# A new slot table for the delta stage of a decoder layer

## The chip, the cores and the metric

The kernel runs on one core of a Trainium2 chip. The core has a matrix engine (TensorE, PE in the profile), a vector engine (VectorE, DVE), an activation engine (ScalarE, ACT), a general engine (GpSimd, POOL) and an engine that issues most transfers (SyncE, SP). Each runs its own instruction list in order and waits on semaphores for the others. The metric is the device time of one execution in microseconds (us); lower is better.

## The reference

The input is x, 4 batches of 1024 tokens of width 256, in float32. One decoder layer is computed: a gated delta-rule attention, a cross attention to a short context, and a mixture of 8 experts with 2 per token, each followed by a layer norm. The change touches only the first part. For every batch and head (4 heads, keys of 64, values of 128) it keeps a state S of 64 x 128 and goes through the tokens:

```python
def _step(S, inp):
    q_t, k_t, v_t, g_t, b_t = inp
    S = S * jnp.exp(g_t)[..., None, None]
    v_eff = (v_t - jnp.einsum('bhk,bhkv->bhv', k_t, S)) * b_t[..., None]
    S = S + k_t[..., None] * v_eff[..., None, :]
    o_t = jnp.einsum('bhk,bhkv->bhv', q_t, S)
    return (S, o_t)
...
o = o * jax.lax.rsqrt(jnp.mean(o * o, -1, keepdims=True) + EPS) * norm_w
o = o * g_out * jax.nn.sigmoid(g_out)
return x + o.reshape(B, T, DV) @ Wo
```

## The kernel before

The kernel is a row of stages with a barrier between them: projections (to about 306 us of the span), the delta stage (to about 872 us), the context, cross attention, experts and the last norm. The delta stage works on chunks of 128 tokens, 8 chunks per batch, the 4 batches side by side. Inside a chunk the recurrence is turned into matrix products with the inverse of a unit triangular 128 x 128 matrix per head.

There is work of two kinds. **Front work** does not need the state. For a chunk it is: turning q and k (`new`, L856; ACT copies them to qkT at L1010), the products k k^T (L834, `kk`), E, the decays between tokens (POOL writes its diagonal at L770, VectorE scans at L1083), PK = kk x E (L1138), the inverse of PK, and PQ = q k^T x E (L834 for `qq`, L1159). The inverse starts with 16 x 16 diagonal blocks: PK's blocks go through DRAM (`lanes`, L692 and L697) to N16, VectorE inverts them (L1101 to L1130), the result goes back through DRAM (`image`, L709, L716, L717) to T and U. Then TensorE doubles the block size in two levels of three groups each: Z (L887, masked by VectorE at L1165), Y (L901, subtracted at L1173) and X (L911, copied by ACT at L1018 or L1022); the last doubling is z6 (L918, copied at L1178) and y6 (L925, copied at L1028).

**The state step** of a batch b in a chunk is the tail: `state_keys` (PE, L941), `targets` (DVE, L1184), `updates` (PE, L949), `updates_out` (ACT, L1034), `outputs` (PE, L957, L961, L967), `new_state` (DVE, L1193), `squares` (ACT, L1041, L1045), `gated` (DVE, L1200, L1205), `gated_turned` (PE, L975), `gated_out` (ACT, L1050), `projected` (PE, L981), `residual` (DVE, L1215 to L1220), `deviations` (ACT, L1054), `norm_terms` (DVE, L1224, L1226), `normed` (ACT, L1058) and `store` (POOL, L798). The PSUM banks A and B exist twice, so batch b uses the pair b % 2, and `state_keys` of b waits until `residual` of b - 2 has read it.

The order on every engine is written out by `run`: a chunk has 16 slots, and in slot f each engine first issues `ready(f)` for chunk c + 1, then `new(f)` for chunk c + 2, then the tails of the four batches for chunk c, then `rest(f)` for chunk c + 2.

```python
for b in sorted(G, key=lambda b: -((f - 4 * b) % SLOTS)):
    n = c - (f < 4 * b)
    if 0 <= n < CHUNKS:
        tail((f - 4 * b) % SLOTS, n, n % 2, b)
```

So batch b starts its step in slot 4b, and a tail phase p of batch b falls into slot 4b + p; of the phases that meet in one slot the oldest batch goes first. Phases 0, 1 and 2 on TensorE are state keys, updates and outputs; in before phase 5 turns the gated output and phase 6 projects it. `ready` and `new` place the front work by slot numbers; `rest` holds the scans and the base inverse.

## Time and profile before

| what | value |
|---|---|
| median of 3 runs | 1945.23 us (1943.38 to 1946.1) |
| the profiled execution | 1951.58 us, of which the span is 1949.8 us |
| TensorE busy in the span | 81% |
| VectorE busy | 59% |
| ScalarE busy | 41% |
| GpSimd busy | 30% |
| granted TensorE clock, mean over the span | 0.893 |

The durations below come from the one profiled execution; the medians come from runs without a profile. Start times are in us from the span's start. A busy TensorE counts the matmuls in flight and is not TensorE at its peak.

### The profile page before, as it was taken

Reading aid. Unit: us, or ns where it says so; the run is one execution under the profiler, and the core shown is the slowest. Engines: PE = TensorE matmul, PEld = TensorE weight load, DVE = VectorE, ACT = ScalarE, POOL = GpSimd, SP = SyncE. Lnnn points to the kernel's source line nnn. Section 1 sums busy time; section 2 is a strip of 40 time slices with the busy share of each in tenths; the row PEclk is TensorE's granted clock in tenths of the full one; section 3 lists DMA queues with packets and bytes.
Section 4 is the critical chain, followed back from the end, with each engine's and each line's share of the span. In section 5 each row is a group of like instructions: output and inputs, shape, how many; then the busy total and the mean of one; then the engine's idle time right before and its main releaser. Section 6 shows DMA issues by size and latency. Waiting matters only on the chain. (4 is left out here: it accounts for less than half of the span.)

```text
span 1949.8 us, 31224 instructions
## 1 busy us (share of the span) xinstructions
PE 1575.8 (81%) x10722; PEld 1115.3 (57%) x10722; DVE 1151.8 (59%) x2425; ACT 807.7 (41%) x1715; POOL 589.1 (30%) x515
## 2 busy tenths in 40 slices
PE   5898982279889898856589999999746999999980
PEld 3444441267778777743347777676633666666650
DVE  4998983356676676323235677777753555554545
ACT  3777771023343434322345555555312333333324
POOL 0222224122132321001023355454542333333330
PEclk9898985578899889977799999999868999999995
DMA  2232326545355543102610222310321111111117
GB/s 83 86 141 85 141 85 163 139 98 140 83 141 149 133 125 96 55 14 104 232 52 32 88 74 76 116 34 23 125 103 29 46 47 47 45 47 48 44 39 261
DMA packets 189896, 178.73 MB, mean 92 GB/s; under 512 B 88392, under 2 KB 148476, under 8 KB 189628
## 3 DMA queue, kind: packets, MB, share of 16 engines
q1 hardware_dynamic: 175131, 149.75, 25.5%
q0 software_dynamic: 10400, 22.95, 3.6%
q10 hardware_dynamic: 4224, 4.19, 0.6%
q8 instruction: 84, 1.38, 0.3%
q14 instruction: 57, 0.46, 0.1%
HBM read 116.73 MB, written 60.11 MB: 91 GB/s over the span
## 5 line engine op out<-in xcount | busy, mean ns | idle before, releaser
L533 DVE SCALAR_TENSOR_TENSOR conv_y<-conv_in,taps,conv_y 128x512 f32<-128x512 f32 x192 | 165.5, 876 | 20.3 <-ACT conv_y L401 15.7
L2231 POOL DMA_INDIRECT y<-o,idx x71 | 83.4, 1175 | 241.9 <-DVE o L2374 234.2
L2310 ACT ACTIVATE xsT<-pX 128x256 f32<-128x256 f32 x71 | 27.3, 384 | 303.7 <-PE pX L2255 303.7
L1674 PE MATMUL xQ<-late,last 128*128 128x512 f32 x256 | 125.3, 612 | 16.5 <-ACT late L1830 7.9
L2266 PE MATMUL pG<-w_gu,xsT 128*128 x284 | 135.5, 600 | 1.3 <-issue 0.6
L2287 PE MATMUL pD<-late,hT 128*128 x568 | 134.2, 379 | 0.0
L2266 PE MATMUL pU<-w_gu,xsT 128*128 x284 | 133.8, 593 | 0.0
L322 PE MATMUL ps_j<-xnT,w_qkv 128*128 128x512 f32 x256 | 132.5, 655 | 0.0
L1640 POOL TENSOR_TENSOR sc<-sc,den 128x1232 f32<-128x1232 f32 x32 | 71.9, 2248 | 174.6 <-DVE den L2056 174.5
L2287 PEld LDWEIGHTS pD<-late,hT 128*128 128x128 f32 x568 | 102.5, 190 | 11.0
L2370 DVE TENSOR_TENSOR o<-pD,late 128x256 f32<-128x256 f32 x71 | 30.2, 425 | 120.8 <-PE pD L2287 120.8
L1634 POOL TENSOR_TENSOR sc<-sc,madd 128x1232 f32<-128x1232 f32 x32 | 82.6, 2581 | 46.1 <-DVE sc L2038 46.1
L2266 PEld LDWEIGHTS pU<-w_gu,xsT 128*128 128x128 f32 x284 | 54.2, 191 | 68.7 <-issue 68.7
L265 POOL TENSOR_TENSOR sq<-tok 128x1024 f32<-128x1024 f32 x16 | 34.2, 2135 | 195.5 <-ACT tok L391 195.5
L2356 DVE TENSOR_TENSOR u<-pU,last 128x512 f32<-128x512 f32 x71 | 49.1, 692 | 67.3 <-issue 50.2
L1625 POOL DMA_INDIRECT list<-ent,idx x64 | 71.3, 1113 | 53.0 <-DVE ent L1995 36.7
L322 PEld LDWEIGHTS ps_j<-xnT,w_qkv 128*128 128x128 f32 x256 | 52.3, 216 | 55.1 <-issue 55.1
L2222 POOL DMA_INDIRECT xs<-x,idx x71 | 68.3, 962 | 45.1 <-DVE idx L2348 24.7
L790 POOL TENSOR_TENSOR ke<-qk,gbt 128x256 f32<-128x256 f32 x32 | 25.7, 804 | 179.8 <-DVE S L1193 179.7
L1674 PEld LDWEIGHTS xQ<-late,last 128*128 128x128 f32 x256 | 45.1, 191 | 59.7 <-issue 31.2
L981 PE MATMUL psAB<-w_o,u 128*128 128x256 f32 x256 | 77.1, 454 | 0.8 <-ACT u L1050 0.8
L1728 PE MATMUL xO<-vw,aT 128*128 128x256 f32 (+1 forms) x320 | 75.6, 393 | 2.3 <-DVE x2t L2066 1.2
(317 smaller groups left out, 3745.2 us busy)
## 6 DMA issues: line engine op xcount, KB each, us to landing
qkvg<-tok SPq DMA_DIRECT2D x8, 2048.0 KB, 6.7
qkvg<-gate SPq DMA_DIRECT2D x8, 1024.0 KB, 8.8
step<-step SPq DMA_DIRECT2D x32, 256.0 KB, 3.8
qk<-qkvg SPq DMA_DIRECT2D x32, 256.0 KB, 4.2
vb<-qkvg SPq DMA_DIRECT2D x32, 256.0 KB
gt<-qkvg SPq DMA_DIRECT2D x32, 256.0 KB
y<-y SPq DMA_DIRECT2D x16, 512.0 KB
xin<-in_x SPq DMA_DIRECT2D x11, 512.0 KB, 4.0
```

Of the source, the lines that this page charges most:

```text
L322: mm = pe.matmul(ps_j[j % 2][:], w_qkv[:, c, j * P:(j + 1) * P], xnT[b][:, c, :], start=c == 0, stop=c == KD - 1)
L533: y = nc.vector.scalar_tensor_tensor(conv_y[m % 4][:], conv_in[b][:, m, k:k + BT], taps[:, m, k:k + 1], conv_y[m % 4][:], ALU.mult, ALU.add)
L981: mm = pe.matmul(B[b % 2][:, 0:D], ogT[b][:, k, :], w_o[:, head(k), :], start=k == 0, stop=k == H - 1)
L1625: nc.gpsimd.indirect_dma_start(out=s["list"], out_offset=bass.IndirectOffsetOnAxis(ap=idx[:, k, t:t + 1], axis=0), in_=ent[:, t, k, :], in ...
L1634: nc.gpsimd.tensor_tensor(v, v, madd[b % 2][:].unsqueeze(1).broadcast_to([P, XH, CTX]), ALU.add).then_inc(masked, 1)
L1640: nc.gpsimd.tensor_tensor(v, v, over_keys(den[g % 2][:]), ALU.mult).then_inc(scaled, 1)
L1674: mm = pe.matmul(Q[:], w_q[:, c, j * P:(j + 1) * P], x1T[:, c, :], start=c == 0, stop=c == KD - 1)
L1728: mm = pe.matmul(O[:, (g % 2) * D:(g % 2 + 1) * D], aT[g % 2][0:rows(c), c, :], vw[b % 2][0:rows(c), c, :], start=c == 0, stop=c == KCH - 1)
L2222: nc.gpsimd.indirect_dma_start(out=xs[q][:], out_offset=None, in_=s["x2"].rearrange("t p d -> (t p) d"), in_offset=bass.IndirectOffsetOnAx ...
L2231: nc.gpsimd.indirect_dma_start(out=s["y"].rearrange("t p d -> (t p) d"), out_offset=bass.IndirectOffsetOnAxis(ap=idx[j % 8][:, 0:1], axis= ...
L2266: mm = pe.matmul(to[:], xsT[q][:, c, :], w_gu[:, bass.ds(e, 1), c, k * FF:(k + 1) * FF], start=c == 0, stop=c == KD - 1)
L2287: mm = pe.matmul(pD[q][:, 0:D], hT[q][:, k, :], w_d[:, bass.ds(e, 1), k, :], start=k == 0, stop=k == FK - 1)
```

## The change

Nothing is computed otherwise, and no buffer is added. Slots and phases are renumbered, and the waits between engines are set to the new order:

| work | slot or phase before | after |
|---|---|---|
| qq products and PQ (c + 1) | 1 | 0 |
| qk turned and copied (c + 2), batches 0, 1 / 2, 3 | 2 / 4 | 1 / 2 |
| kk products and PK (c + 2) | 5 | 4 |
| Z, Y, X of level 4 (c + 1) | 3, 7, 8 | 5, 6, 8 |
| Z, Y, X of level 5 | 9, 10, 11 | 9, 10, 12 |
| scans of the four batches | 1, 2, 3, 4 | 0, 1, 2, 3 |
| base inverse (m = 1, 2, 4, 8) | 8, 9, 9, 10 and 11 | 8, 8, 9, 10 and 11 |
| diagonals out, in; inverses out | 6, 8; 11 | 5, 7; 12 |
| loads of the next scores | 5, 9, 13, 15 | 4, 8, 11, 15 |
| gated output turned, copied | phase 5 | phase 6 |
| projected and residual | phase 6 | phase 7 |
| deviations, norm terms, normed, store | 7, 8, 9, 10 | 8, 9, 10, 11 |

The waits: turning qk of the second pair now waits on PQ of the chunk before (before: on Z), kk no longer waits on Z, Z of level 4 waits on PK of the next chunk for all batches, and Y of level 4 no longer does.

```diff
@@ -634,7 +634,7 @@
         at = lambda c, b: c * BATCH + b + 1
         LEVS, SLOTS = (4, 5), 16
         lat = lambda c, lev, b: (c * len(LEVS) + lev - LEVS[0]) * BATCH + b + 1
-        Z_AT, Y_AT, X_AT = {3: 4, 9: 5}, {7: 4, 10: 5}, {8: 4, 11: 5}
+        Z_AT, Y_AT, X_AT = {5: 4, 9: 5}, {6: 4, 10: 5}, {8: 4, 12: 5}
         FIRST, SECOND = (0, 1), (2, 3)
         flat = lambda t: t[:].rearrange("p k j -> p (k j)")
         lanes, image = s["lanes"], s["image"]
@@ -725,11 +725,11 @@
                 load_scores(b, c + 1 + b * CHUNKS)
 
             def new(f, c, par):
-                if f == 6:
+                if f == 5:
                     diagonals_out(c, par)
-                if f == 8:
+                if f == 7:
                     diagonals_in(c)
-                if f == 11:
+                if f == 12:
                     inverses_out(c)
                 if f == 15:
                     inverses_in(c)
@@ -737,8 +737,8 @@
                         for b in G:
                             load_values(b, 0)
                             load_gates(b, 0)
-                if c + 1 < CHUNKS and f in (5, 9, 13, 15):
-                    next_scores((5, 9, 13, 15).index(f), c)
+                if c + 1 < CHUNKS and f in (4, 8, 11, 15):
+                    next_scores((4, 8, 11, 15).index(f), c)
 
             def tail(f, c, par, b):
                 if c + 1 == CHUNKS:
@@ -746,7 +746,7 @@
                 if f == 1:
                     sp.wait_ge(w_done, at(c, b))
                     load_values(b, c + 1)
-                if f == 7:
+                if f == 8:
                     sp.wait_ge(x_sum, at(c, b))
                     load_gates(b, c + 1)
 
@@ -798,19 +798,16 @@
                 pool.dma_start(s["x1"][c + b * CHUNKS], x1t[b][:]).then_inc(x1_out[b], 16)
 
             def new(f, c, par):
-                if f == 1 and c:
+                if f == 0 and c:
                     for b in G:
                         diagonal(c, b)
                 if f % 4 == 3:
                     if c:
                         key_ends(c, f // 4, par)
-                    if f > 3:
-                        decayed(c, f // 4, par)
-                if f == 4:
-                    decayed(c, 0, par)
+                    decayed(c, f // 4, par)
 
             def tail(f, c, par, b):
-                if f == 10:
+                if f == 11:
                     store(c, b)
 
             for b in G:
@@ -843,28 +840,23 @@
                     round_of(pair, 1).then_inc(done, 1)
 
             def new(f, c, par):
-                if f in (2, 4):
-                    for b in (FIRST, SECOND)[f // 4]:
+                if f in (1, 2):
+                    for b in (FIRST, SECOND)[f - 1]:
                         pe.wait_ge(qk_in[b], c * 80 + 80)
                         if c:
-                            if b in FIRST:
-                                pe.wait_ge(pq_done, at(c - 1, b))
-                            else:
-                                pe.wait_ge(z_sb, lat(c - 1, LEVS[0], b))
+                            pe.wait_ge(pq_done, at(c - 1, b))
                             pe.wait_ge(qkg_done, at(c - 1, b))
                         for k in range(4):
                             mm = pe.transpose(M[b][:, k * P:(k + 1) * P], qk[b][:, k * P:(k + 1) * P], ident)
                         mm.then_inc(qkT_done, 1)
-                if f == 5:
+                if f == 4:
                     def free(pair):
                         pe.wait_ge(qkT_sb, at(c, pair[1]))
-                        if c and pair == FIRST:
-                            pe.wait_ge(z_sb, lat(c - 1, LEVS[0], pair[1]))
 
                     products(c, 1, free, kk_half, kk_done)
 
             def ready(f, c, par):
-                if f == 1:
+                if f == 0:
                     def free(pair):
                         pe.wait_ge(pk_done, at(c, pair[1]))
                         if c:
@@ -876,8 +868,8 @@
                     for b in G:
                         if lev == LEVS[0]:
                             pe.wait_ge(t_in, c * 16 + 16)
-                            if b in FIRST and c + 1 < CHUNKS:
-                                pe.wait_ge(qkT_sb, at(c + 1, b))
+                            if c + 1 < CHUNKS:
+                                pe.wait_ge(pk_done, at(c + 1, b))
                             else:
                                 pe.wait_ge(pq_done, at(c, b))
                         else:
@@ -894,8 +886,6 @@
                         pe.wait_ge(z_sb, lat(c, lev, b))
                         if lev == LEVS[0]:
                             pe.wait_ge(u_in, c * 16 + 16)
-                            if c + 1 < CHUNKS:
-                                pe.wait_ge(pk_done, at(c + 1, b))
                         for k in range(H):
                             for r in HALF:
                                 mm = pe.matmul(M[b][half(r), P + k * (HP // 2):P + (k + 1) * (HP // 2)],
@@ -989,9 +979,9 @@
                     updates(c, par, b)
                 if f == 2:
                     outputs(c, par, b)
-                if f == 5:
+                if f == 6:
                     gated_turned(c, b)
-                if f == 6:
+                if f == 7:
                     projected(c, b)
 
             run(new, ready, tail)
@@ -1002,8 +992,8 @@
             act.wait_ge(set_up, 3 + 3 * BATCH)
 
             def new(f, c, par):
-                if f in (2, 4):
-                    for b in (FIRST, SECOND)[f // 4]:
+                if f in (1, 2):
+                    for b in (FIRST, SECOND)[f - 1]:
                         act.wait_ge(qkT_done, at(c, b))
                         if c:
                             act.wait_ge(qkg_done, at(c - 1, b))
@@ -1063,11 +1053,11 @@
                     updates_out(c, b)
                 if f == 3:
                     squares(c, b)
-                if f == 5:
+                if f == 6:
                     gated_out(c, b)
-                if f == 7:
+                if f == 8:
                     deviations(c, b)
-                if f == 9:
+                if f == 10:
                     normed(c, b)
 
             run(new, ready, tail)
@@ -1131,21 +1121,22 @@
                                       X16[:, 0:LANE].rearrange("p (r c) -> p c r", r=B0)).then_inc(base_done, 1)
 
             def new(f, c, par):
-                if f == 5:
+                if f == 4:
                     for b in G:
                         dve.wait_ge(kk_done, c * 2 + b // 2 + 1)
                         dve.wait_ge(E_done, at(c, b))
                         nc.vector.tensor_tensor(flat(PK[par][b]), M[b][:], flat(E[b]), ALU.mult).then_inc(pk_done, 1)
 
             def rest(f, c):
-                if f in (1, 2, 3, 4):
-                    decays(c, f - 1)
+                if f in (0, 1, 2, 3):
+                    decays(c, f)
                 if f == 8:
                     first_blocks(c)
+                    upper_left(2)
+                    lower_right(2)
                 if f == 9:
-                    for m in (2, 4):
-                        upper_left(m)
-                        lower_right(m)
+                    upper_left(4)
+                    lower_right(4)
                 if f == 10:
                     upper_left(8)
                 if f == 11:
@@ -1153,7 +1144,7 @@
                     last_blocks()
 
             def ready(f, c, par):
-                if f == 1:
+                if f == 0:
                     for b in G:
                         dve.wait_ge(qq_done, c * 2 + b // 2 + 1)
                         nc.vector.tensor_tensor(flat(PQ[par][b]), M[b][:], flat(E[b]), ALU.mult).then_inc(pq_done, 1)
@@ -1233,9 +1224,9 @@
                     new_state(c, par, b)
                 if f == 4:
                     gated(c, b)
-                if f == 6:
+                if f == 7:
                     residual(c, b)
-                if f == 8:
+                if f == 9:
                     norm_terms(c, b)
 
             run(new, ready, tail, rest)
```

## Rows read from the trace of the kernel before

**Rows 1.** Windows, chunks 1 to 5: length, busy us per engine, clock, DMA share, GB/s.

```profile
476.36:764.32 287.96, 256.70 (x3682) 225.62 (x3682) 195.51 (x535) 112.11 (x360) 80.59 (x100) 0.92 0.48 124
```

**Rows 2.** Waits in the same stretch: total us, times, longest.

```profile
PE psAB L975 <- DVE w L1205: 18.9, 13, 2.4
DVE X L1101 <- DMA N<-lanes: 15.4, 5, 4.3
...
PE psM L901 <- DVE Z L1165: 8.1, 5, 2.8
```

**Rows 3.** Timeline (start, us), TensorE, last matmuls of a step (L967).

```profile
475.70 0.66 PE L967 MATMUL psAB<-u,ke 128*64 128x128 f32 x8
...
709.24 0.66 PE L967 MATMUL psAB<-u,ke 128*64 128x128 f32 x8
...
719.56 0.66 PE L967 MATMUL psAB<-u,ke 128*64 128x128 f32 x8
...
731.57 0.66 PE L967 MATMUL psAB<-u,ke 128*64 128x128 f32 x8
...
763.66 0.66 PE L967 MATMUL psAB<-u,ke 128*64 128x128 f32 x8
```

**Rows 4.** Timeline, TensorE and VectorE, the step from batch 3 to batch 0.

```profile
709.95 0.61 DVE L1193 SCALAR_TENSOR_TENSOR S<-S,late,psAB 128x128 f32<-128x128 f32 x2 [1.23 <-PE psAB L967]
...
710.37 1.95 PE L834 MATMUL psM<-qkT 64*128 64x128 f32 x32
...
712.15 0.18 DVE L1200 RECIPROCAL ssum<-ssum 128x4 f32<-128x4 f32 x1 [1.34 <-ACT ssum L1045]
...
713.41 0.67 DVE L1184 TENSOR_TENSOR w<-vb,psAB 128x512 f32<-128x512 f32 x1
...
714.00 2.47 DVE L1159 TENSOR_TENSOR PQ<-psM,E 128x512 f32<-128x512 f32 x4
...
715.13 1.04 PE L856 MATMUL psM<-con,qk 128*128 128x128 f32 x8
...
716.01 1.89 PE L981 MATMUL psAB<-w_o,u 128*128 128x256 f32 x8
```

**Rows 5.** Timeline, POOL, the diagonal of batch 3 that waits for qk.

```profile
719.91 1.04 POOL L770 TENSOR_TENSOR E<-gbt,con 128x512 f32<-128x512 f32 x1 [1.13 <-DMA qk<-qkvg]
```

**Rows 6.** Timeline, VectorE, from batch 0 to batch 1.

```profile
717.94 0.42 DVE L1215 SCALAR_TENSOR_TENSOR x1t<-xr,psAB 128x256 f32<-128x256 f32 x1
...
718.86 0.18 DVE L1220 BATCH_NORM_AGGREGATE mv<-stats 128x2 f32<-128x6 f32 x1
...
720.79 1.24 DVE L1083 TENSOR_TENSOR_SCAN E<-step,E 128x512 f32<-128x512 f32 x1
...
722.73 2.14 DVE L1083 TENSOR_TENSOR_SCAN E<-step,E 128x512 f32<-128x512 f32 x1
...
728.02 2.46 DVE L1138 TENSOR_TENSOR PK_<-psM,E 128x512 f32<-128x512 f32 x4
```

**Rows 7.** Timeline, base inverse on VectorE, and y6 on TensorE twice.

```profile
691.51 1.03 DVE L1113 TENSOR_TENSOR V<-X,N 128x512 f32<-128x512 f32 x1
...
696.01 0.38 DVE L1130 COPY XT<-X 128x256 f32<-128x256 f32 x1
...
700.75 3.67 PE L925 MATMUL psM<-UF,U 64*64 64x64 f32 x32
...
809.16 2.12 PE L925 MATMUL psM<-UF,U 64*64 64x64 f32 x32
```

**Rows 8.** Timeline, the beginning and the end of the stage.

```profile
431.12 1.04 POOL L770 TENSOR_TENSOR E<-gbt,con 128x512 f32<-128x512 f32 x1 [4.00 <-DMA qk<-qkvg]
...
440.84 0.66 PE L967 MATMUL psAB<-u,ke 128*64 128x128 f32 x8
...
825.83 0.66 PE L967 MATMUL psAB<-u,ke 128*64 128x128 f32 x8
...
836.52 0.66 PE L967 MATMUL psAB<-u,ke 128*64 128x128 f32 x8
```

## The prediction

> **What bounds the kernel now.** I began with the page: TensorE is the busiest engine, but over eight stages an average share says little, and the change touches one stage only. So I cut the delta stage out with the windows view. Five whole chunks (chunk 1 to chunk 5) take 287.96 us, 57.6 each; TensorE is busy for 89% of that, VectorE for 68%, and TensorE's granted clock averages 0.92 [rows 1]. A mean of 0.92 between the levels 2.4 and 1.2 GHz says that for 16% of the time, about 9 us of each chunk, the matmuls ran at the lower level. The reader is to see that neither engine is full, so order decides.
>
> Next the waits. Inside this stretch TensorE idles 18.9 us in front of the turning of the gated output (L975), 13 times, because VectorE has not yet written it, and 8.1 us in front of L901, because VectorE stands at L1101 waiting for the 16x16 blocks from DRAM [rows 2]. Both are VectorE's in-order queue, seen from TensorE.
>
> Then the timeline. The state update (L967) ends each batch's step, so the distance between its ends is the length of a step: from 709.90 (709.24 + 0.66) it is 10.3 to batch 0, 12.0 to batch 1 and 32.1 for batches 2 and 3 together [rows 3]. Step by step the chain is the same: L967, new_state, squares, gated(b-1), targets(b), updates(b), outputs(b). targets(b) does not need gated(b-1), it only stands behind it in VectorE's queue. So what bounds a step is everything that VectorE has queued between new_state(b-1) and targets(b), or TensorE's own work in the step, whichever is longer.
>
> **The unit costs** [rows 4]: new_state ends 0.66 after L967; keys of the state 0.5 (709.90 to 710.37); one round of products (qq or kk) 1.95; reciprocal to the end of targets 1.93 (712.15 to 714.08); updates 1.05 (714.08 to 715.13); PQ, four multiplications, 2.47; two batches turned (L856) 1.04, so one set of four 0.5, as the gated output is; projection 1.89; outputs 2.3 (717.90 to 720.22). Residual with its statistics 1.10, one decay scan 1.24 to 2.14, PK 2.46 [rows 6]. The base inverses' second half (L1113 to L1130) 4.88, a group of 64x64 matmuls for four batches 2.1 at full clock [rows 7].
>
> **Check on before, at full clock.** b0: new_state, squares and gate to 4.2, updates 1.1, turning 0.7, projection 1.9, outputs 2.3 = 10.3, measured 10.3. b1: measured 12.0. b2: X 2.1, keys 0.5, Z 2.1, turning 0.5, updates 1.1, Y 2.1, projection 1.9, outputs 2.3, plus 8.1/5 = 1.6 of wait [rows 2] = 14.2. b3: 0.66 + 4.88 + norm terms 0.4 + 1.93 = 7.9, then updates 1.1, y6 2.1, projection 1.9, outputs 2.3 = 15.3. Sum 51.8; measured 57.6. The 5.8 us that remain I put down to the lower clock: y6 took 3.67 us in one chunk and 2.12 in another [rows 7].
>
> **The change, part by part.** No instruction is added or removed; each engine's order changes. The gain is real: between updates(b) and outputs(b) the projection (1.9) gives way to the turning (0.5) and a front group, and the turning, where TensorE idled, no longer stands before updates(b). But VectorE's queue between new_state(b-1) and targets(b) grows. I sum each step from the end of L967.
>
> *b3 to b0.* PQ moves from slot 1 to slot 0, where ready() runs ahead of the tails, so its four multiplications stand in front of gated(b3) and targets(b0); so does residual(b2). Projection to 1.9, first pair of products by 3.5, PQ to 6.0, gate and targets to 7.9, updates to 9.1. Then the second pair of qk is turned, now slot 2 instead of 4, ahead of outputs(b0). Batch 3's qk comes by a chain that the change does not shorten: new_state, key_ends, decayed, the loads, the DMA. In before POOL waits for it until 719.91, 10.0 after L967's end; the five chunks give 10.0 to 13.0, mean 11.0 [rows 5]. So: 11.0, turned 12.0, gated output 12.5, outputs 14.9 (rounded up for handoffs). Before 10.3.
>
> *b0 to b1.* new_state 0.66, decays(2), residual(b3), decays(3), PK (moved from slot 5 to 4, again ahead of the gate): 0.66 + 1.6 + 1.1 + 1.6 + 2.46 = 7.5 with small gaps, gate and targets 9.5, updates 10.7, Y 2.1 to 12.8, turning 0.5, outputs 2.3 = 15.6. Before 12.0. In before two scans and the four small masks stood here, but PK did not.
>
> *b1 to b2.* VectorE has only residual(b0) and the gate, 5.5; TensorE has 1.9 + 2.1 + 0.5 + 2.1 + 1.1 + 2.1 + 0.5 + 2.3 = 12.6, say 12.7, and sets the length. The blocks come in time: PK ends some 8 us before this step begins, so the waits at L1101 (15.4 us in five chunks) and L901 [rows 2] go. Before 14.2.
>
> *b2 to b3.* 0.66 + 4.88 + residual 1.1 + 1.93 = 8.6, updates 9.8, y6 11.9, turning, outputs: 14.8. Before 15.3.
>
> Sum 58.0 against 51.8. TensorE's idle time per chunk at full clock is now 10 us (58.0 less its work of 48.0, worked out under A) where before it was 6.3 (57.6 less 256.7/5) [rows 1], so I see no reason for the clock to fall less often; but part of what it costs now falls into waits. I take 3.5 us per chunk, between 0 (full clock) and 5.8 (as before): 61.5, +3.9 per chunk, five chunks +19.7.
>
> *Price of the scans.* Both moved scans run while POOL makes key_ends and decayed of batch 0; the scan takes 1.24 or 2.14 us [rows 6]. I take 1.6, the ends give -0.7 and +1.1 per chunk. The Trainium skill (SBUF — State Buffer, section SBUF: two separate sides) says that VectorE with two SBUF inputs and GpSimd exclude each other for a whole instruction; by that both scans would take the long time and five chunks cost 5 us more. The two durations agree with it.
>
> *Start.* Batch 3's qk of chunk 2 came at 431.12 [rows 8]; the loads of batch 2, some 2.7 us of issuing, now go ahead of the image writes, so about 428.5. In before outputs(b0) of chunk 0 did not wait for it; now they do: 432, then 15.6: 447.6, against 441.50 for b1 in before [rows 8], +6. Chunk 0's b2 and b3 give back 3.5. Net +2.5.
>
> *End.* Without front work a step goes projection and residual to 3.1, gate and targets 1.93, updates 1.1, the copy of u beside the turning (I take 0.9), outputs 2.3 = 9.3, against 10.7 (826.49 to 837.18) [rows 8]: three such steps -4.2. Chunk 6 has half the front work: b0 7.9 + 1.1 + 0.5 + 2.3 = 11.8, b1 5.0 + 1.1 + 2.1 + 0.5 + 2.3 = 11.0, b2 and b3 12.7 each by TensorE's work; with chunk 7's first step 57.5 against 62.2 from 764.32 to 826.49 [rows 3, 8], -4.7. Of these 8.9 I leave 3 to the lower clock: -6.
>
> Total +19.7 + 2.5 - 6 = +16. The profiled execution took 1951.58 (span 1949.8 and 1.8 around it), so it would become 1968; it lay 6.3 above the median of 1945.23, and by the median I forecast 1962.
>
> **Rivals.** *A, faster: TensorE is the bound.* Its work per chunk is 4 x 6.3 + 3.9 + 2.1 + 16.8 = 48.0; with the clock's 5.8 that is 53.8, five chunks -19, with the ends 1923. For it: the waits before L975 [rows 2] are exactly what the new order fills. Against it: it needs VectorE to reach the end of targets within 5.4 us in b0 and 6.5 in b1; the queue gives 7.9 and 9.5. It decides where those fall below TensorE's 5.4 and 6.5.
>
> *B, no change: full clock.* If the evener spread kept the clock at 2.4 GHz, chunks take 58.0, five of them +2, start and end -3.5: 1944; with the scans at their short price 1940.
>
> *C, the clock is lost as often as before or more.* 58.0 + 5.8 to 8: 1973 to 1984. The Trainium skill (TensorE: Matmul & The Clock Gate, section HAM oscillation) describes short bursts between waits that fall back to the lower clock again and again; by that rule, with more waits than before, the time is that of C. The 3.67 against 2.12 us of y6, behind an idle time of 2.4, agrees.
>
> *D, the qk of batch 3 is in time.* If it were there by 9.1, b0 would be 13.0, five chunks -9.5: 1952, still slower. For it: the DMA lands at 10.0 in some chunks [rows 5]; against it: nothing starts it earlier.
>
> **The numbers.** Forecast with D 0.60; C 0.13; A 0.13; B 0.14, which lies on both sides of no change. A measurement here tells apart 0.2%, 3.9 us. Slower 0.74, same 0.12, faster 0.14. The range runs from B's lower end to between C's ends, 1943 to 1979; the forecast's own is 1950 to 1972.
>
> **What would show it.** L967's ends: b0 near 15 instead of 10.3, b1 near 15.6, b2 shorter; VectorE's PQ directly in front of the gate; TensorE waiting at L856 for the DMA of qk; the wait before L975 gone and one before updates in its place; a chunk of about 61. Wrong if b0 stays under 12, or if the mean clock rises above 0.95.

## The result, and the profile after

The changed kernel takes 1970.33 us (median of 4 runs, 1966.98 to 1981.23) against 1944.31 for the kernel before on the same chip: 1.016 times as long, interval 1.0097 to 1.0223. It is 26 us slower. The forecast was 1962 with 1950 to 1972 as its own range. One run among the experiments below (experiment 11, 2898.8 us at a clock of 0.632, where its five others have 0.90 to 0.91) was in a slower state and stands in no ratio.

The profiled execution took 1981.23 us, its span is 1979.4, the mean clock 0.884. Nearly all of the loss is in the delta stage: it ran from 306 to 872 us and now runs to 901, 29 of the 30 us between the two profiled executions. Five whole chunks and each step of the fourth of them in the windows view, columns as in [rows 1]:

```profile
473.21:797.75 324.54, 283.06 (x3682) 244.81 (x3681) 183.76 (x535) 111.37 (x360) 77.09 (x100) 0.85 0.43 112
664.00:682.00 18.00, 13.51 (x101) 11.30 (x102) 8.45 (x20) 5.78 (x17) 6.54 (x8) 0.81 0.62 183
682.00:700.80 18.80, 16.70 (x213) 14.57 (x213) 10.67 (x27) 3.50 (x13) 3.27 (x4) 0.76 0.40 92
700.80:714.20 13.40, 13.25 (x245) 11.56 (x245) 8.80 (x39) 5.04 (x17) 2.47 (x4) 0.95 0.34 111
714.20:727.70 13.50, 12.67 (x183) 11.10 (x181) 8.84 (x22) 7.92 (x25) 3.14 (x4) 1.00 0.37 75
```

The reader is to see two things. A chunk takes 64.9 us (324.54 / 5) where it took 57.6 [rows 1]. And it is lost in two steps: b0 and b1 have grown to 18 and 19 us, at a clock of 0.81 and 0.76, while TensorE in b0 is busy for only 13.5 of 18 us. Steps b2 and b3 are short and full. The means over chunks 1 to 5, from the ends of the last matmul of each step:

| step | before | forecast, full clock | after |
|---|---|---|---|
| b0 | 10.4 | 14.9 | 18.3 |
| b1 | 12.5 | 15.6 | 19.2 |
| b2 | 16.8 | 12.7 | 13.0 |
| b3 | 17.9 | 14.8 | 14.4 |
| chunk | 57.6 | 58.0, and 3.5 for the clock | 64.9 |

Waits of the same stretch (total us, times, longest), to lay beside [rows 2]:

```profile
POOL E L770 <- DMA qk<-qkvg: 29.3, 5, 6.8
...
PE psAB L939 <- DVE w L1175: 21.4, 15, 2.4
...
PE psM L850 <- DMA qk<-qkvg: 14.4, 5, 4.5
...
PE psM L879 <- DVE PK_ L1128: 5.0, 5, 1.0
```

The 15.4 us that VectorE waited for the blocks at L1101 and the 8.1 us of TensorE behind them are gone. The 18.9 us in front of the turning are gone too, and 21.4 us stand in front of the updates (now L939) in their place. New is L850: once in each chunk TensorE waits 2.9 us on average for the DMA of batch 3's q and k, and GpSimd 5.9 for the same transfer at L770. Before Z of level 4 (L879) TensorE waits 1.0 us a chunk for PK. The step to batch 0 shows where (timeline, TensorE, VectorE and GpSimd):

```profile
663.34 0.66 PE L957 MATMUL psAB<-u,ke 128*64 128x128 f32 x8
...
665.50 1.26 POOL L781 TENSOR_TENSOR qkgT<-qkT,grow 128x512 f32<-128x512 f32 x1
...
667.51 2.48 DVE L1150 TENSOR_TENSOR PQ<-psM,E 128x512 f32<-128x512 f32 x4 [0.46 <-PE psM L831]
...
669.92 0.17 DVE L1191 RECIPROCAL ssum<-ssum 128x4 f32<-128x4 f32 x1
...
671.16 0.68 DVE L1175 TENSOR_TENSOR w<-vb,psAB 128x512 f32<-128x512 f32 x1
...
671.89 2.08 PE L939 MATMUL psAB<-w,UF 128*128 128x128 f32 x8 [2.36 <-DVE w L1175]
...
676.95 0.66 PE L850 MATMUL psM<-con,qk 128*128 128x128 f32 x4 [2.13 <-DMA qk<-qkvg]
676.98 1.04 POOL L770 TENSOR_TENSOR E<-gbt,con 128x512 f32<-128x512 f32 x1 [5.59 <-DMA qk<-qkvg]
...
680.98 0.94 PE L957 MATMUL psAB<-u,ke 128*64 128x128 f32 x8
```

From 664.00: PQ ends at 6.0 and the targets at 7.84 (forecast 6.0 and 7.9). Then the q and k of batch 3 come at 12.95, where 11.0 was forecast and 10.0 was measured before [rows 5]. The outputs stand behind them. The same stretch on SyncE's queue, which issues the transfers, says why they are late. Its 16 writes of the base inverses (image) wait for VectorE's last copy, to XT:

```profile
655.65 0.38 DVE L1120 COPY XT<-X 128x256 f32<-128x256 f32 x1
```

```profile
654.02 0.33 SPq L666 DMA_DIRECT2D gbt<-gb  x1
...
656.92 0.43 SPq L672 DMA_DIRECT2D qk<-qkvg  x1
657.47 3.79 SPq L709 DMA_DIRECT2D image<-X  x8
661.30 5.15 SPq L709 DMA_DIRECT2D image<-XT  x8
666.49 0.45 SPq L678 DMA_DIRECT2D gt<-qkvg  x1
...
668.00 0.42 SPq L716 DMA_DIRECT2D T<-image  x1
668.47 0.43 SPq L717 DMA_DIRECT2D U<-image  x1
669.08 0.32 SPq L666 DMA_DIRECT2D gbt<-gb  x1
...
671.35 0.43 SPq L672 DMA_DIRECT2D qk<-qkvg  x1
```

SyncE issues with no gap over 0.2 us from 654.02 to the load of batch 3's q and k, issued by 671.78. The 16 writes take 9.0 us, and batch 3's loads, which need GpSimd's L781 to be done (666.76), cannot start before 669.08, 2.3 us late. Before, the same queue of SyncE in the same chunk:

```profile
696.41 3.81 SPq L709 DMA_DIRECT2D image<-X  x8
700.26 3.88 SPq L709 DMA_DIRECT2D image<-XT  x8
...
712.72 0.32 SPq L666 DMA_DIRECT2D gbt<-gb  x1
```

There the writes were issued 5.8 us before the step b3 ended (704.14 against 709.90), SyncE then stood idle from 709.42, and batch 3's loads started 2.8 us behind the step's end, right behind GpSimd. Now the writes end 2.4 us behind it (666.45 against 664.00). Which of two things did this, the loads of batch 2 that now go ahead of the writes (slot 11, before 13) or the shorter step b3, is taken up behind the experiments.

In the step to batch 1 the forecast order is there as well (same view, VectorE and TensorE):

```profile
686.48 2.45 DVE L1128 TENSOR_TENSOR PK_<-psM,E 128x512 f32<-128x512 f32 x4
...
690.09 0.68 DVE L1175 TENSOR_TENSOR w<-vb,psAB 128x512 f32<-128x512 f32 x1
...
690.82 1.16 PE L939 MATMUL psAB<-w,UF 128*128 128x128 f32 x8 [1.09 <-DVE w L1175]
...
691.91 3.63 PE L891 MATMUL psM<-Z,U 64*64 64x32 f32 x64
...
699.67 1.12 PE L957 MATMUL psAB<-u,ke 128*64 128x128 f32 x8
...
709.26 2.06 PE L891 MATMUL psM<-Z,U 64*64 64x32 f32 x64 [0.15 <-DVE Z L1156]
```

PK stands in front of the targets, which end 8.85 us after 681.92 (forecast 9.5). What follows was to take 6.1 us and takes 10.0: the group L891 needs 3.63 us here and 2.06 at 709.26, in a step whose clock is 0.95. That is the lower level, not a wait.

### The profile page after: what moved, and what is told of

Same layout as the page of the kernel before. It is cut to its first block and busy times, and to the rows that moved or that the text cites. A ratio compares the mean times of both kernels' runs of the same rounds, so it can differ in the third digit from the quotient of the medians.

```text
span 1979.4 us, 31222 instructions
## 1 busy us (share of the span) xinstructions
PE 1600.1 (81%) x10722; PEld 1131.0 (57%) x10722; DVE 1137.8 (57%) x2425; ACT 805.5 (41%) x1715; POOL 587.5 (30%) x515
## 5 line engine op out<-in xcount | busy, mean ns | idle before, releaser
L533 DVE SCALAR_TENSOR_TENSOR conv_y<-conv_in,taps,conv_y 128x512 f32<-128x512 f32 x192 | 165.4, 876 | 19.9 <-ACT conv_y L401 15.3
L1665 PE MATMUL xQ<-late,last 128*128 128x512 f32 x256 | 127.2, 620 | 16.5 <-ACT late L1821 7.8
L1184 DVE SCALAR_TENSOR_TENSOR S<-S,late,psAB 128x128 f32<-128x128 f32 x64 | 19.4, 345 | 158.9 <-PE psAB L957 158.9
L790 POOL TENSOR_TENSOR ke<-qk,gbt 128x256 f32<-128x256 f32 x32 | 28.2, 880 | 253.0 <-DVE S L1184 253.0
L850 PE MATMUL psM<-con,qk 128*128 128x128 f32 x128 | 26.9, 354 | 84.0 <-DMA qk<-qkvg 69.5
L322 PEld LDWEIGHTS ps_j<-xnT,w_qkv 128*128 128x128 f32 x256 | 52.2, 215 | 54.9 <-issue 54.9
```

The source lines that it names most:

```text
L322: mm = pe.matmul(ps_j[j % 2][:], w_qkv[:, c, j * P:(j + 1) * P], xnT[b][:, c, :], start=c == 0, stop=c == KD - 1)
L533: y = nc.vector.scalar_tensor_tensor(conv_y[m % 4][:], conv_in[b][:, m, k:k + BT], taps[:, m, k:k + 1], conv_y[m % 4][:], ALU.mult, ALU.add)
L1665: mm = pe.matmul(Q[:], w_q[:, c, j * P:(j + 1) * P], x1T[:, c, :], start=c == 0, stop=c == KD - 1)
```

## The experiments

"Steps" are again the means of chunks 1 to 5 of the profiled execution, b0 / b1 / b2 / b3. Ratios are to the kernel before on the same chip. Experiments 1 to 4 ran on one chip, 5 to 8 on a second, 9 to 12 on a third; the kernel before took 1942.19, 1946.52 and 1943.1 to 1943.51 us there, so that a difference in us between two experiments on different chips can be off by 4 us, and the ratios say it better.

**1. The change again.** No edit.

> The changed kernel once more, as the reference for the runs beside it. My theory (VectorE's queue and the late qk of batch 3 lengthen the steps of batches 0 and 1) and the rival (the lower clock alone makes the loss) both expect 1.3% over before, some 25 us, with steps of 18, 19, 13 and 13.5 us.

1974.89 us, 1.016 (1.0133 to 1.0188). The result stands; the loss is a little over the 1.3% expected. Steps 17.8 / 18.4 / 13.0 / 15.3, chunk 64.5: b3 took 18.0 and 18.1 us at a clock of 0.72 in two of the five chunks and 13.5 in the others.

**2. Only the tails.** Before, with its front table, but the gated output turned at phase 6 and all that follows one phase later.

```diff
-                if f == 5:
+                if f == 6:
                     gated_turned(c, b)
-                if f == 6:
+                if f == 7:
                     projected(c, b)
```

> The kernel before with the phases of the tails alone moved (turning of the gated output, projection, residual and what follows a slot later); the slot table of the front work stays. By my sums at full clock: b0 10.2 (was 10.3), b1 12.7 (12.0), b2 14.8 (14.2), b3 16.2 (15.3), because the projection now stands behind a front group and the residual behind it delays the gate; +2 per chunk, -4 at the end: 0.3% slower, 1950. A rival in which the tails' move is the good part of the change expects 1930 or less (the wait before the turning, 3.8 us per chunk, gone).

1937.55 us, 0.997 (0.9949 to 0.999): faster by 0.3%, where slower by about as much was expected; the 1930 of the rival was not reached either. Steps 9.8 / 12.5 / 14.6 / 18.9, chunk 55.9, and the last two chunks 90.5 instead of 96.1 us. The tails' move is the good half of the change.

**3. Only the fronts.** After, with the tails' phases of before (the reverse of the edit above).

> The changed kernel with the tails' phases of before: the new slot table of the front work alone. By my sums the projection returns between updates and outputs, 1.9 us in every step, which the shorter wait before the gate does not give back in b0 (bound by the late qk) and b1: 62 per chunk at full clock, about 0.5% above the changed kernel (1980). A rival in which the tails' move is what costs expects it at the time of before, 1945.

1997.66 us, 1.0279 (1.0247 to 1.0311). Steps 15.7 / 18.4 / 13.0 / 19.2, chunk 66.2, last two chunks 101.9; slower by more than expected. So in the new front table the tails' move is worth 23 us, and the new front table is what costs. (I had expected 1980.)

**4. The turning of batches 2 and 3 one slot later.** After, with the second pair of q and k turned and copied in slot 3, behind outputs(b0), instead of slot 2.

```diff
-                if f in (1, 2):
-                    for b in (FIRST, SECOND)[f - 1]:
+                if f in (1, 3):
+                    for b in (FIRST, SECOND)[f // 2]:
```

> The changed kernel with one edit: qk of batches 2 and 3 is turned and copied in slot 3 instead of 2, behind outputs(b0) and ahead of the projection. If the late qk of batch 3 holds outputs(b0) up, the step to b0 goes from 18 to about 12.5 us, the step to b1 grows by about 1, and the time falls by 10 to 25 us against the changed kernel (1945 to 1960). If TensorE's clock or VectorE's queue alone make the loss, it stays within 5 us of the changed kernel.

1941.7 us, 0.9995 (0.9972 to 1.0019). This one edit takes back 33 us, all that the change lost and more than the 10 to 25 expected. Steps 12.4 / 18.6 / 12.9 / 13.5, chunk 57.3. PQ and PK still stand where the change put them. Two steps b1 in the windows view, the same instructions:

```profile
592.30:608.50 16.20, 13.88 (x221) 12.07 (x221) 10.24 (x27) 4.58 (x15) 3.78 (x5) 1.00 0.57 144
646.90:668.40 21.50, 18.04 (x221) 15.57 (x221) 10.25 (x27) 4.58 (x15) 3.48 (x5) 0.78 0.50 132
```

16.2 us at full clock, 21.5 at 0.78: VectorE's work is the same to 0.01 us. Of the 5.3 us between them 1.15 are a longer wait of TensorE for batch 3's q and k, which now stand in this step (1.82 us against 0.67); the 4.16 us more that TensorE is busy are the lower clock.

**5. TensorE kept busy in the waits.** After, with the four transposes of batches 1 and 2 issued four and five times over, so that TensorE has work where it idled.

```diff
-                        for k in range(4):
+                        for k in [*range(4)] * (1, 4, 5, 1)[b]:
```

> The changed kernel, in which TensorE turns qk of batch 1 four times and that of batch 2 five times in place of once, with the same result, so that its waits before updates(b0) (2.4 us) and for batch 3's qk (about 2 us) are filled. If the idle time is what brings the clock down behind it, the low stretches in the steps to b0 and b1 go, the steps fall from 18 and 19 to about 16.5 and 16, and the time by 10 to 20 us against the changed kernel (1955 to 1965). If the clock falls for another reason, the steps stay within 0.5 us or grow by what is filled in too much.

1982.11 us, 1.0177 (1.0136 to 1.0218). The fill did not close the waits: 1.05 us remained before the updates and 2.28 before the q and k. The updates ran at the higher level (1.16 us instead of 2.08), and b1 was at the lower one again:

```profile
667.30:685.60 18.30, 14.97 (x129) 12.80 (x129) 8.42 (x19) 5.79 (x17) 6.53 (x8) 0.91 0.61 179
685.60:703.70 18.10, 16.06 (x215) 14.20 (x213) 10.64 (x27) 3.50 (x13) 3.27 (x4) 0.81 0.43 97
```

The forecast fall of 10 to 20 us did not come. As the waits were not closed, this does not settle what brings the clock down, and it gives no support to filling. It shows another thing: steps b3 and b0 came as 17.9 and 14.5 or as 13.5 and 18.4, some 32 us together either way. That is taken up below.

**6. X of level 5 later.** The kernel of experiment 2 with one more cell of the new table.

```diff
-        Z_AT, Y_AT, X_AT = {3: 4, 9: 5}, {7: 4, 10: 5}, {8: 4, 11: 5}
+        Z_AT, Y_AT, X_AT = {3: 4, 9: 5}, {7: 4, 10: 5}, {8: 4, 12: 5}
```

> The kernel before with the tails' phases of the change and one more edit of its table: X of level 5 in slot 12 in place of 11, so that the projection of batch 1 goes first and the residual no longer delays the base inverse and the gate. By my sums the step to b3 falls from 18.9 (in the kernel with the tails alone) to about 14 and its low clock goes with the wait of 1.8 us: a chunk of 51 to 52, 1.2 to 1.5% below before (1913 to 1920). The rival, that the b3 step is bound by VectorE's base inverse wherever X stands, expects no difference from the kernel with the tails alone (1937).

1921.6 us, 0.9876 (0.9838 to 0.9914). Steps 9.7 / 16.1 / 14.6 / 14.4, chunk 54.7: b3 is 4.5 us shorter than in experiment 2, and b1, where the clock was down in three chunks, 3.5 longer. So the time is just above the 1913 to 1920 expected, and the chunk well above 51 to 52: TensorE waits 7.7 us in the five chunks for the transfer to T (L716), which the expectation does not have.

**7. PK twice.** Experiment 4's kernel with every multiplication of PK issued twice.

```diff
+                        link(nc.vector.tensor_tensor(flat(PK[par][b]), M[b][:], flat(E[b]), ALU.mult))
```

> The changed kernel with the second pair turned in slot 3, and each of the four PK multiplications made twice, with the same result (2.6 us more on VectorE per chunk). If VectorE's queue ahead of the gate sets the step to b1, that step grows by 2.5 to 2.8 from 16.1 and 19.4, and the others stay. If TensorE or the clock sets it, it grows by less than 0.5.

1970.99 us (two runs), 1.0126 (1.0064 to 1.0187). Step b1 grew by 4.5 us, to 23.1, where 2.5 to 2.8 were expected; b0, b2 and b3 stayed at 12.8 / 13.0 / 13.5. 2.5 us of that is the doubled work; the rest goes with the clock, which now was low in b1 of every chunk (0.67 to 0.74; in experiment 4 in three of five). So in b1 VectorE's queue ahead of the targets sets the length; how much of the growth is the clock's own is not separated.

**8. PQ twice.** After, with every multiplication of PQ issued twice, in the step b0.

```diff
+                        link(nc.vector.tensor_tensor(flat(PQ[par][b]), M[b][:], flat(E[b]), ALU.mult))
```

> The changed kernel with each PQ multiplication made twice (2.6 us more on VectorE, ahead of the gate, in the step to b0). If the qk of batch 3, 12.9 us behind the end of the step before, sets the step to b0, nothing changes there (at most 1 us: updates then end near 12). If VectorE's queue sets it, the step grows by 2.6 from 18.

1971.87 us (two runs), 1.013 (1.0069 to 1.0192): the 2.5 us more in VectorE's queue cost nothing. b0 took 17.0 to 17.7 us, and the q and k came 12.6 to 13.8 us behind the step before. In b0 VectorE is not what is waited for.

**9. Z of level 4 behind the tails.** Experiment 6's kernel; TensorE and VectorE issue Z and its masks behind the tails of slot 3 instead of ahead of them.

```diff
+                    if behind and f == 3 and 0 <= c + 1 < CHUNKS:
+                        behind(f, c + 1, (c + 1) % 2)
...
+                if f in Z_AT and f != 3:
+                    first_z(f, c, par)
```

> The kernel of e5 with Z of level 4 and its masks issued behind the tails of slot 3 on TensorE and VectorE, so that the projection and residual of batch 3 go first and T's transfer (TensorE waits 1.9 us per chunk for it in e5) has the time of the projection. If TensorE's order in the step to b1 counts, that step falls by 2 to 3 us, and by more where its clock no longer falls: 1900 to 1912 against 1921 for e5. If the step to b1 is set by VectorE's scans alone, within 3 us of e5.

1915.16 us, 0.9855 (0.9821 to 0.9888). Steps 9.8 / 14.3 / 14.7 / 13.5, chunk 52.2; the first step b1 of the stage, 21.6 in experiment 6, stayed at 22.0, of which TensorE waits 8.2 for T. The 1900 to 1912 expected was not reached. Against experiment 6 it is 6 us, and the intervals of the two ratios overlap: that Z's place is worth anything is not shown.

**10. Eight writes on another queue.** After, with nothing changed but who issues the eight XT writes of the base inverses: GpSimd in slot 12, not SyncE.

```diff
-                for k, t in enumerate((X16, XT16)):
+                for k, t in ((0, X16),):
...
+            def inverses_out(c):
+                pool.wait_ge(base_done, c + 1)
...
+                        pool.dma_start(image[k, part, :, lo:lo + B0].rearrange("r u c -> u r c"),
+                                       t[part, 0:LANE].rearrange("u (r c) -> u r c", r=B0)).then_inc(img_two, 16)
```

> The changed kernel with the eight writes of XT to DRAM issued by GpSimd in place of SyncE. SyncE issues without a gap from the loads of batch 2's next scores to the end of batch 3's. If SyncE's queue makes batch 3's qk late (12.9 us behind the step, 11.0 forecast), its loads start 2 us sooner, right behind decayed, and the step to b0 falls by 1.5 to 2 us: 5 to 12 us less than the changed kernel (1963 to 1970). If the DMA engines or POOL's chain set it, no difference, or slower.

1948.5 us, 1.0015 (0.9988 to 1.0041), 26 us less than experiment 1, where 5 to 12 were expected. From its timeline, the end of step b3 to that of b0:

```profile
638.60 4.49 POOL L807 DMA_DIRECT2D image<-XT  x8 [1.85 <-DVE XT L1137]
...
645.62 0.66 PE L973 MATMUL psAB<-u,ke 128*64 128x128 f32 x8
...
649.10 0.32 SPq L666 DMA_DIRECT2D gbt<-gb  x1
...
656.09 1.38 POOL L771 TENSOR_TENSOR E<-gbt,con 128x512 f32<-128x512 f32 x1 [2.42 <-DMA qk<-qkvg]
...
659.95 0.66 PE L973 MATMUL psAB<-u,ke 128*64 128x128 f32 x8
```

and from its waits, over five chunks:

```profile
PE psM L866 <- DMA qk<-qkvg: 1.8, 3, 0.8
```

Batch 3's loads start 2.8 us after the step's end instead of 5.1, its q and k come at 9.8 instead of 12.95, TensorE's wait for them falls from 14.4 to 1.8 us, and b0 takes 13.4 to 14.4 us. Over the five chunks they come 10.1 us behind the step's end on average, 3.2 sooner than after, not the 2 us expected; the clock of b0 is 0.88 to 1.00, after it was 0.74 to 0.91. b1 remains at 18.0 to 19.8. The Trainium skill (DMA: Bandwidth & Descriptors, section Issuing engines are not separate DMA queues) says that issuing from several engines saves only the sequencer's time, usually small beside the transfer; here, where transfers wait behind one another to be issued, it was 5.2 us of SyncE's for the eight writes of the chunk shown above, and taking them off that queue was worth 26.

**11. Both.** Experiment 9's kernel with experiment 10's edit.

> The kernel of e8 with XT's writes on GpSimd as in e9. T lands about 4 us sooner, which counts only if TensorE still waits for it in e8; there it should be hidden behind the projection. I expect within 3 us of e8; if e8 still waits for T, up to 6 us less.

1897.27 us (median of all 6), 0.9751 (0.9714 to 0.9788), the lowest median of all. It is 18 us below experiment 9, where 6 at most were expected: TensorE's wait for T in the first step b1 falls from 8.2 to 0.9 us, and b1 runs at a clock of 1.00 in all five chunks. Steps 9.7 / 12.1 / 14.7 / 15.3, first step b1 11.5. Chunks 1 to 5:

```profile
457.66:716.82 259.16, 248.18 (x3681) 216.91 (x3681) 187.61 (x535) 109.62 (x360) 102.65 (x140) 0.96 0.55 145
```

TensorE is busy 96% of it, 89% before.

**12. Without experiment 9's edit.** Experiment 6's kernel with the eight writes on GpSimd.

> The kernel of e5 with XT's writes on GpSimd, without the edit of e8: which of the two makes e10 fast. If SyncE's queue is what counts, it lies within 5 us of e10 (1897 to 1903), TensorE no longer waits for T, and the first step to b1 (22 us in e8, 11.5 in e10) is short. If both edits are needed, it lies at e8 or above (1912 to 1920).

1902.54 us, 0.978 (0.9749 to 0.9812). Steps 9.7 / 12.7 / 14.7 / 14.4. In the chunks TensorE no longer waits for T, as expected; in the first step b1 it still does, for 3.8 us, and that step takes 17.9, not the short one expected. Against experiment 6 the eight writes are worth 19 us. The interval overlaps that of experiment 11, so that Z's place is worth anything once the writes are moved is not shown either. Experiments 4 and 10, each of which takes the wait out of the changed kernel, were not put together.

## Why the prediction was right, and where its sizes were off

Direction, range and the chain in each step held. Four signs came: PQ in front of the gate, TensorE waiting at the turning of q and k, the wait that moves from the turning of the gated output to the updates, a shorter b2. Three sizes did not: b0 near 15 (18.3), b1 near 15.6 (19.2), a chunk of 61 (64.9). The range was held narrowly: 1970.33 lies 2 us inside it, experiment 1 with 1974.89 outside. The stage grew by 28.2 us in the profiled executions (end of the last step at 888.65, before 860.4) where 16 was forecast:

- *Five chunks: +36.6, forecast +19.7.* Three terms were mis-sized. **Batch 3's q and k** were put at 11.0 and came at 12.95 in the chunk read here, +1.9 (13.2 on average over the five). I took over the mean of before, "a chain that the change does not shorten", and did not sum SyncE's queue against the length of b3, although I forecast a b3 of 14.8 where it had been 17.9. The passage below has the rows. **The clock** was put at 3.5 us a chunk. It cost 1.1 in b0 (4.97 us from the q and k to the end, forecast 3.9), 3.9 in b1 (10.0 against 6.1) and 0.9 in b3 (one of five took 18.1), 5.9 in all: the size of rival C. **b3** was 1.3 too long: 13.5 at full clock. The targets, forecast 8.6 us into b3, ended at 7.4 (657.87 against 650.52). With 0.65 less in b1 (below) and 0.3 more in b2 that makes +2.7 a chunk of the +3.4 missed; the rest is that the two steps read here are 0.7 below their means.
- *VectorE's queue.* In b0 it was sized right (7.84 for 7.9) and decided nothing: experiment 8 lengthened it for nothing. In b1 it was 0.65 too long and does decide: experiment 7. Experiment 4 keeps PQ and PK in their new places and is as fast as before: what VectorE's queue costs in b1 is no more than the rest of the change gains. I had named that queue the main reason for slower, and it is not.
- *Which half.* I did not forecast the halves apart, and when I did, for experiment 2, I had the sign wrong: the old order's b2 and its last chunks held lost time that the tails' move gives back. Experiments 2 to 4 and 10 put the loss in one place: the front table turns batch 3's q and k ahead of outputs(b0), before SyncE has them there. Experiments 4 and 10 take this wait away by different edits and each bring the time back to that of before.
- *The scans* were taken at 1.6 us. They took 1.22 to 1.66, median 1.22, in the 20 scans of five chunks (before: median 1.55). In b3 the second multiplication of the base inverse took 1.00 instead of 1.95 us, since the residual now stands between it and GpSimd's L781: it starts at 717.60 and GpSimd ends at 717.66; before it started at 693.30 with GpSimd running to 694.37. The Trainium skill (SBUF — State Buffer, section SBUF: two separate sides) has the two exclude each other. 694.37 and 1.00 give the measured end of 695.25 to 0.12. In all five chunks it took 1.00 after and 1.95 to 1.97 before, and with the tails' old phases in the new table (experiment 3) it took 1.95 or 1.96 again. This makes up about 1.0 of the 1.3 us by which b3 was forecast too long. It does not make b3 short by itself: in experiment 2 it took 0.99, and b3 18.9.
- *Start: -3.2, forecast +2.5.* The first b1 ended at 446.97 as forecast (447.6), but by luck: b0 ended 2.9 us sooner than I had it (429.15 for 432), and b1 took 17.8 us for 15.6. b2 and b3 then took 26.2 us where I had 31.4, because before had lost more there than my sums at full clock showed.
- *End: -5.2, forecast -6.*

**The rivals.** *A* needed VectorE at the targets within 5.4 us and did not get it. *B* asked for a clock that did not come. *C*: its size of the clock term came (5.9 a chunk, a mean clock of 0.85 instead of 0.92). The Trainium skill (TensorE: Matmul & The Clock Gate, section HAM oscillation) tells of bursts of matmuls that are shorter than the wait behind them; that is not this case, as TensorE is busy for 16.7 of the 18.8 us of the step b1 above, and no run here shows that rule at work. The row that I called in agreement with it does not bear it out, either. Both of the y6 groups of [rows 7] stand behind the same idle time, and one took 3.67 us and the other 2.12:

```profile
698.00 1.11 PE L975 MATMUL psAB<-con,w 128*128 128x128 f32 x4 [2.40 <-DVE w L1205]
...
806.40 1.11 PE L975 MATMUL psAB<-con,w 128*128 128x128 f32 x4 [2.40 <-DVE w L1205]
```

What in the order brings the clock down stays open, as experiment 5 closed none of the waits. *D*, q and k in time, was worked out at 1952; experiment 10, which brings them at 9.8, took 1948.5.

**Why the q and k come late.** In the kernels before, after and of experiments 1, 5 and 6 VectorE has the base inverse done 5.4 to 5.5 us behind the *start* of b3, however long b3 is. Only then can SyncE issue the 16 writes, the transfers to T and U and batch 3's loads. Batch 3's loads also need GpSimd's L781, which is done 2.8 us behind the *end* of b3. So a shorter b3 leaves SyncE less time for its queue. The chunks of these kernels, with the time at which the q and k are there (the start of GpSimd's L770 that waits for them):

| chunks | b3 just before | q and k, from b3's start | from its end | b0 |
|---|---|---|---|---|
| before, five | 16.4 to 19.8 | 29.0 to 30.6 | 10.0 to 13.0 | 10.3 to 10.5 |
| after, five | 13.5 | 25.5 to 27.7 | 12.0 to 14.2 | 16.9 to 19.7 |
| experiment 1, behind a long b3 | 18.1 | 28.4 | 10.3 | 13.7 |
| experiment 5, three | 17.9 to 18.0 | 27.9 to 28.4 | 10.0 to 10.5 | 14.4 to 14.6 |
| experiment 5, two | 13.5 | 26.7, 27.0 | 13.2, 13.5 | 18.1, 18.4 |
| experiment 6, four | 13.5 | 27.7 to 30.0 | 14.2 to 16.5 | 9.7 |

The chunk of experiment 1, whose order is that of the changed kernel: the loads start 2.8 us behind the step's end (665.67), and the q and k come in time for a b0 of 13.7 us.

```profile
664.76 0.91 PE L957 MATMUL psAB<-u,ke 128*64 128x128 f32 x8
...
668.50 0.32 SPq L666 DMA_DIRECT2D gbt<-gb  x1
...
676.01 1.04 POOL L770 TENSOR_TENSOR E<-gbt,con 128x512 f32<-128x512 f32 x1 [2.95 <-DMA qk<-qkvg]
```

A chunk of experiment 6, where batch 2's loads still go behind the writes and b3 is short: batch 3's loads start 6.5 us behind the step's end (578.53), and the q and k come at 15.7. It costs b0 nothing, because there the outputs do not stand behind them.

```profile
574.39 4.93 SPq L709 DMA_DIRECT2D image<-XT  x8
...
577.87 0.66 PE L967 MATMUL psAB<-u,ke 128*64 128x128 f32 x8
...
585.05 0.58 SPq L666 DMA_DIRECT2D gbt<-gb  x1
...
594.25 1.04 POOL L770 TENSOR_TENSOR E<-gbt,con 128x512 f32<-128x512 f32 x1 [4.63 <-DMA qk<-qkvg]
```

So the reader is to see that the new place of batch 2's loads is not what makes the q and k late; counted from the start of b3 they come sooner after than before. What makes them late is b3's own gain: it ends 5.1 us sooner in these chunks (13.5 for 18.6 on average), and the q and k only 2.9. It is also why a low clock in b3 costs the changed kernel next to nothing: the longer b3 comes back as a shorter b0.

**Still open:** why b1 runs at the lower level in most chunks and not in all, in kernels as in experiment 4, where the order is the same in each. The wait for the q and k is not needed for it: in experiment 10 it is all but gone, and b1 ran at 0.68 to 0.81 in all five chunks.

## What to carry to other kernels

Sum the queue of the engine that issues transfers as you sum a computing engine's: instruction by instruction, from the event that lets it start. Where that event hangs on the start of a step and the consumer on its end, every us that the step gains is one that the queue loses. A consumer that is moved ahead in an in-order queue brings its transfer onto the path; before asking how fast the transfer is, ask what else is waiting to be issued. And time the parts of a renumbered table by themselves: here one half gained, the other lost, and either one cell of the table or eight small writes on another queue brought the loss back.

## What the runs showed of the hardware

- Small writes are dear to issue: 16 strided writes held SyncE for 9.0 us (3.79 and 5.15 for eight) in the chunk shown and 7.7 to 9.5 in the ten chunks of before and after, most single loads of the same stretch 0.32 to 0.59. Eight of them took GpSimd 4.49 us, on an engine that had the time.
- TensorE was busy 13.9 us with the instructions of one step at a granted clock of 1.00 and 18.0 at 0.78; a group of 64 small matmuls took 2.06 and 3.63. The 4.2 us in one step are more than experiments 2, 6 or 9 took off a whole chunk (1.7, 1.2 and 2.5).
- Giving TensorE more transposes before a wait went with a higher clock in that step (0.91 for 0.81) and no gain in time (1.0177 against 1.016).
- The two-input multiplication of 128x512 on VectorE took 1.00 us when GpSimd's product L781 ended 0.06 us behind its start, and 1.95 when L781 ran over its first 1.07 us.
